# A decoder layer on one core: in the first batch the last four heads' queries come straight from the loaded weights in float32, and GpSimd splits three of the four output weight pieces

## The reference

```python
# 1: attention with 16 query heads, 4 key/value heads, D = 128, window 128
q, k, v = x @ q_kernel, x @ k_kernel, x @ v_kernel      # 256 -> 2048, 512, 512
q, k = apply_rope(q, sin, cos), apply_rope(k, sin, cos)
scores = einsum(q_block, [k_before, k_own]) / sqrt(D), masked
out = einsum(softmax(scores), [v_before, v_own]) @ out_kernel   # 2048 -> 256
x = layernorm(x + out)
# 2: a 256 x 256 attention of the context with itself, applied to x
x = layernorm(x + x_m)
# 3: mixture of experts, 2 shared and 16 routed with the best 4, hidden width 176
x = layernorm(x + moe(x))
```

## Time and profile before

| | us |
|---|---|
| median of 3 runs | 394.87 (394.62 to 395.32) |
| the profiled execution, its own time | 394.55 |
| its span in the profile | 392.8 |
| PE busy | 380.9 (97%) |
| DVE, ACT, POOL busy | 282.9, 264.6, 195.7 |

### The profile page before, as it was taken

One profiled execution on the slowest core, in us unless ns is written; L12 is line 12 of the kernel. 1 busy time (PEld: TensorE's weight loads), 2 busy tenths in 40 slices (PEclk: granted clock), 3 DMA queues, 4 the chain that ended last, 5 costly groups with the idle time before them and its releaser, 6 DMA issues.

```text
span 392.8 us, 8296 instructions
## 1 busy us (share of the span) xinstructions
PE 380.9 (97%) x2520; PEld 342.5 (87%) x2520; DVE 282.9 (72%) x781; ACT 264.6 (67%) x660; POOL 195.7 (50%) x334
## 2 busy tenths in 40 slices
PE   8899899999999999999999999999999999999995
PEld 5767789989999989999998978888889998999995
DVE  4989998778879767978778866765857536645455
ACT  5899887777687777687768785765766644544443
POOL 1598665744777645676546654787856100000000
PEclk9999999999999999999999999999999999999999
DMA  7631500000010000000000494322223222243321
GB/s 262 204 110 48 194 26 4 3 0 3 0 30 0 0 0 0 0 0 0 0 0 1 133 374 163 99 97 81 82 83 94 69 70 78 97 143 99 92 63 53
DMA packets 16709, 28.04 MB, mean 71 GB/s; under 512 B 2198, under 2 KB 7816, under 8 KB 16680
## 3 DMA queue, kind: packets, MB, share of 16 engines
q1 hardware_dynamic: 16248, 27.03, 21.3%
q10 hardware_dynamic: 432, 0.66, 0.5%
HBM read 26.57 MB, written 1.11 MB: 70 GB/s over the span
## 4 chain that ended last, share of the span: by engine, by line
PE 85%; DVE 6%; issue 3%; ACT 2%; POOL 2%; DMA 2%; DVEq 0%; ACTq 0%; POOLq 0%
PE bank L724 22%; PE bank L725 22%; PE bank L726 22%; PE bank L869 6%; PE bank L879 5%; PE bank L868 3%; PE bank L826 2%; PE bank L820 1%; DMA xraw<-in_xt 1%; DVE by_sin L1363 1%; DVE by_cos L1362 1%; POOL nprobs L1600 1%; PE bank L834 1%; DMA raw_q<-in_pieces 1%; POOL nprobs L1599 0%
## 5 line engine op out<-in xcount | busy, mean ns | idle before, releaser
L1030 ACT ACTIVATE hid<-bank,small_sb 128x512 f32<-128x512 f32 x48 | 33.0, 687 | 56.0 <-PE bank L726 47.4
L1250 DVE TENSOR_TENSOR hid<-hid,gate_rows 128x512 f32<-128x512 f32 (+1 forms) x44 | 31.8, 724 | 48.3 <-ACT hid L1030 48.1
L725 PE MATMUL bank<-w_lo,hid_hi 128*128 128x256 f32 (+1 forms) x200 | 56.4, 282 | 0.0
L1591 POOL TENSOR_TENSOR queryT<-by_cos,by_sin 128x512 f32<-128x512 f32 x32 | 41.2, 1287 | 17.1 <-DVE by_sin L1363 16.3
L1599 POOL TENSOR_SCALAR nprobs<-probs,rsums 128x128 f32<-128x128 f32 x64 | 24.5, 383 | 49.6 <-DVE rsums L1379 35.3
L1233 DVE TENSOR_TENSOR hid_lo<-hid,hid_hi 128x512 fp32r<-128x512 f32 x48 | 36.1, 753 | 5.4 <-ACT hid_hi L1051 5.4
L726 PE MATMUL bank<-x2T_hi,w_lo 128*128 128x512 f32 (+1 forms) x100 | 39.5, 395 | 0.0
L725 PEld LDWEIGHTS bank<-w_lo,hid_hi 128*128 128x128 f32 (+1 forms) x200 | 37.7, 188 | 2.0
L869 PE MATMUL bank<-keyT,queryT 128*128 128x256 f32 x128 | 38.2, 381 | 0.0
L724 PE MATMUL bank<-xT_hi,wq_hi 128*128 128x256 f32 x124 | 37.0, 298 | 1.3 <-issue 1.3
L1233 DVE TENSOR_TENSOR pT_lo<-bank,pT_hi 128x384 fp32r<-128x384 f32 x64 | 35.0, 547 | 4.0 <-ACT pT_hi L1126 4.0
(11 more groups left out here) (168 smaller groups left out, 1238.3 us busy)
## 6 DMA issues: line engine op xcount, KB each, us to landing
stage<-in_pieces SPq DMA_DIRECT2D x8, 512.0 KB, 4.3
w_raw<-in_w SPq DMA_DIRECT2D x4, 1024.0 KB, 12.2
gate_rows<-gates_d SPq DMA_DIRECT2D x16, 256.0 KB, 3.1
gate_rows<-gates_d SPq DMA_DIRECT2D x8, 224.0 KB, 3.0
w_raw<-in_w SPq DMA_DIRECT2D x2, 768.0 KB, 7.6
gate_rows<-gates_d SPq DMA_DIRECT2D x8, 192.0 KB, 2.9
gate_rows<-gates_d SPq DMA_DIRECT2D x8, 160.0 KB, 2.4
xraw<-in_xt SPq DMA_DIRECT2D x4, 256.0 KB, 3.1
```

The lines of the kernel that those rows point to most:

```text
L725: nc.tensor.matmul(o, sh, ml, start=False, stop=False, **kw)
L1030: nc.scalar.activation(hid[:, u % 2, :], z_bank[u % 3][:], ACT.Relu, bias=b1_cols[:, i % NC:i % NC + 1]).then_inc(relu_done, 1)
L1250: nc.vector.tensor_tensor(own, own, gate_rows[rows, i % 3, :], ALU.mult).then_inc(gated, 1)
L1591: nc.gpsimd.tensor_tensor(o.rearrange("p a t -> p (a t)"), by_cos[:, r % 2, :], by_sin[:, r % 2, :], ALU.add).then_inc(rope_add, 1)
```

## The change

1. `RAW` gains q6 and q7 (heads 12 to 15). In the first batch each is 4 float32 products of 256 columns of the loaded q3 piece and `xraw`, in place of 12 split products. Other batches still use the split weights.
2. The q3 piece's split moves from between heads 4 and 5 to behind head 8, and its low part goes from POOL to DVE.
3. POOL makes the low parts of o1, o2 and o3, two instructions each; DVE made them before. DVE keeps o0.
4. `load_piece` waits for the raw slots before it loads o3 into q3's buffer, and o3 is loaded after o2. `raw_read` now means q7.
5. The first loads change order (q2 before the second cross transfer), some steps of the first batch change places, and the second warm-up product has 256 columns in place of 384.

```diff
-FIRST_AT = {"act": {"e": 3.719, ..., "piece q3": 4.88, ..., "heads_hi1 0": 9.4995, ...
+FIRST_AT = {"act": {"e": 4.528, ..., "heads_hi1 0": 8.332, ...
-RAW = {"q0": "q0a", "k0": "ka"}
+RAW = {"q0": "q0a", "k0": "ka", "q6": "q3", "q7": "q3"}
-PIECE_AT = {..., "kb": -0.785, ..., "q3": 4.957, "o0": 6.587, "o1": 8.1, "o2": 10.128, "o3": 12.478}
+PIECE_AT = {..., "kb": -0.218, ..., "o0": 6.587, "o1": 7.995, "q3": 8.6, "o2": 8.893, "o3": 12.1}
-LOADS = ["tables", "q0b", "cross 0", "q1", "kb", "cross 1", "q2", "ident", "v", "small", "q3", "o1", "o0", "o3", "o2"]
+LOADS = ["tables", "q0b", "cross 0", "q1", "kb", "q2", "ident", "cross 1", "v", "small", "q3", "o1", "o0", "o2", "o3"]
-LOW_AT = {"v": (2.6, 2.9), "q3": (4.6, 4.8)}
+LOW_AT = {"v": (2.6, 2.9), "o1": (8.6, 9.4), "o2": (10.3, 10.8), "o3": (12.299999999999999, 12.6)}
@@ raw_slot
-            for a in range(2):
+            for a in range(first, first + 2):
                 for k in range(KC):
-                    mm = nc.tensor.matmul(o[:, a * T:(a + 1) * T], w[:, k, a * D:(a + 1) * D], xraw[:, k, :],
+                    mm = nc.tensor.matmul(o[:, (a - first) * T:(a - first + 1) * T], w[:, k, a * D:(a + 1) * D], xraw[:, k, :],
@@ load_piece
+            if n >= 6 and SOURCES[n - 4] in RAW.values():
+                raw_read(sp)
@@ slot on PE
-                    mm = raw_slot(e, o, RAW[s])
+                    mm = raw_slot(e, o, RAW[s], 0 if RAW[s] in HALVES else 2 * (j % 2))
@@
-            keep_busy(512, 384)
+            keep_busy(512, 256)
```

More of the change, by code:

```diff
@@ L114 @@
 }
-FIRST_AT = {"act": {"e": 3.719, "probs_hi 0": 3.077, "q0": -1.712, "v0": 5.9842, "exp 7": 8.009, "exp 8": 8.994, "q3": 0.963, "x": -4.174, "q6": 7.6425, "exp 4": 5.093, "q7": 10.714, "q1": -0.719, "probs_hi 9": 12.249, "q4": 4.991, "v1": 5.765, "k0": -1.004, "probs_hi 7": 10.211, "exp 5": 5.108, "exp 9": 10.073, "probs_hi 4": 6.488, "probs_hi 2": 5.1005, "probs_hi 5": 7.368, "cross 1": 5.9585, "exp 0": 0.87, "piece q3": 4.88, "probs_hi 1": 4.436, "probs_hi 3": 6.212, "piece o1": 8.064, "probs_hi 6": 10.065, "piece o2": 10.371, "exp 1": 1.82, "k1": 1.904, "piece q0b": -1.89, "piece q0a": -2.328, "heads_hi1 0": 9.4995, "piece v": 2.374, "q2": -0.505, "piece ka": -2.22, "exp 6": 7.069, "piece kb": -0.7595}, "dve": {"e": 2.182, "e recip": 2.532, "q0": -1.661, "recip 0": 0.951, "v0": 6.036, "top 0": -0.427, "q3": 1.198, "q6": 8.014, "q4": 4.902, "probs_lo 6": 9.5865, "q7": 10.714, "piece q2": 1.022, "q1": -0.719, "top 4": 2.927, "recip 4": 5.305, "probs_lo 4": 6.596, "top 9": 8.057, "recip 2": 2.516, "probs_lo 9": 12.249, "cross 1": 5.752, "heads_lo1 0": 8.42, "v1": 5.901, "k0": -1.288, "top 6": 5.221, "probs_lo 2": 4.981, "top 2": 1.208, "probs_lo 1": 3.313, "probs_lo 5": 7.706, "top 5": 4.042, "recip 5": 5.306, "top 10": 9.433, "top 1": 0.087, "probs_lo 3": 6.212, "probs_lo 7": 10.025, "recip 1": 1.438, "top 8": 7.617, "recip 8": 8.959, "piece v": 2.059, "heads_lo0 0": 7.37, "k1": 1.847, "probs_lo 0": 2.524, "piece kb": -0.8735, "q2": -0.339, "cross 0": -0.7492, "recip 6": 6.714, "recip 9": 9.5098, "piece o2": 10.09, "top 7": 6.118, "recip 7": 7.833, "piece q0a": -2.857, "recip 3": 3.895}, "pool": {"e copy": -0.151, "normalise 0": 0.494, "q0": -1.555, "k1": 2.094, "q3": 1.95, "normalise 7": 7.651, "q6": 8.0868, "e norm": 4.64, "q7": 10.714, "q1": -0.735, "normalise 9": 9.076, "q4": 5.538, "normalise 4": 4.798, "normalise 3": 2.61, "normalise 1": 1.275, "normalise 8": 9.023, "k0": -1.288, "normalise 2": 2.448, "normalise 5": 5.013, "x": -2.99, "normalise 6": 6.54, "q3 0": 5.4615, "v 1": 2.524, "q2": -0.505, "q5": 7.037}, "pe": {"q0": -1.207, "score 6": 5.0, "v0": 5.866, "q3": 1.371, "q6": 7.899, "e": 3.4688, "score 8": 8.381, "q7": 10.714, "out0 0": 9.857, "q1": -0.719, "v1": 5.807, "turn 9": 12.249, "q4": 4.991, "score 7": 5.01, "values1 0": 9.184, "k0": -1.08, "score 5": 4.312, "score 4": 3.723, "score 2": 2.303, "turn 1": 4.797, "turn 6": 9.096, "score 3": 3.576, "turn 4": 7.014, "turn 2": 5.02, "score 9": 9.122, "turn 5": 7.351, "score 0": 0.11, "score 1": 1.078, "turn 3": 6.212, "cross 1": 2.483, "k1": 1.98, "turn 0": 3.54, "score 10": 9.714, "q2": -0.505, "q5": 7.173, "turn 7": 9.7855}}
@@ new lines @@
+FIRST_AT = {"act": {"e": 4.528, "probs_hi 0": 2.805, "q0": -1.712, "v0": 5.9842, "exp 7": 8.009, "exp 8": 8.994, "q3": 0.963, "x": -4.174, "q6": 7.858, "exp 4": 5.093, "q7": 10.272, "q1": -0.719, "probs_hi 9": 12.249, "q4": 4.991, "v1": 5.765, "k0": -1.004, "probs_hi 7": 10.211, "exp 5": 5.108, "exp 9": 10.073, "probs_hi 4": 6.488, "probs_hi 2": 5.1005, "probs_hi 5": 7.368, "cross 1": 5.9585, "exp 0": 0.87, "probs_hi 1": 4.436, "probs_hi 3": 6.212, "piece o1": 8.064, "probs_hi 6": 10.065, "piece o2": 10.371, "exp 1": 1.82, "k1": 1.961, "piece q0b": -1.89, "piece q0a": -2.328, "heads_hi1 0": 8.332, "piece v": 0.9165, "q2": -0.289, "piece ka": -2.22, "exp 6": 7.069, "piece kb": -0.7595, "q5": 7.413}, "dve": {"e": 2.991, "e recip": 3.341, "q0": -1.661, "recip 0": 0.951, "v0": 6.036, "top 0": -0.427, "q3": 1.198, "q6": 8.229, "q4": 4.902, "probs_lo 6": 9.5865, "q7": 10.272, "piece q2": 1.022, "q1": -0.501, "top 4": 2.927, "recip 4": 5.305, "probs_lo 4": 6.938, "top 9": 8.057, "recip 2": 2.516, "probs_lo 9": 12.249, "cross 1": 5.752, "heads_lo1 0": 8.42, "v1": 5.901, "k0": -1.288, "top 6": 5.221, "probs_lo 2": 4.981, "top 2": 1.208, "probs_lo 1": 3.313, "probs_lo 5": 7.706, "top 5": 4.03, "recip 5": 5.306, "top 10": 9.433, "top 1": 0.087, "probs_lo 3": 6.212, "probs_lo 7": 10.025, "recip 1": 1.438, "top 8": 7.617, "recip 8": 8.959, "piece v": 2.059, "heads_lo0 0": 7.37, "k1": 1.935, "probs_lo 0": 2.252, "piece kb": -0.8735, "q2": -0.123, "cross 0": -0.7492, "recip 6": 6.714, "recip 9": 9.636, "piece o2": 10.09, "top 7": 6.063, "recip 7": 7.833, "piece q0a": -2.487, "recip 3": 3.895}, "pool": {"e copy": 0.658, "normalise 0": 0.494, "q0": -1.667, "k1": 3.228, "q3": 1.95, "normalise 7": 7.859, "q6": 8.302, "e norm": 5.449, "q7": 10.272, "q1": -0.735, "normalise 9": 10.286, "q4": 5.236, "normalise 4": 4.798, "normalise 3": 2.61, "normalise 1": 1.275, "normalise 8": 9.023, "k0": -1.288, "normalise 2": 2.448, "normalise 5": 5.088, "x": -2.99, "normalise 6": 6.54, "q3 0": 5.4615, "v 1": 2.524, "q2": -0.289, "q5": 7.037}, "pe": {"q0": -1.18, "score 6": 5.0, "v0": 5.866, "q3": 1.371, "q6": 8.114, "e": 4.278, "score 8": 9.109, "q7": 10.272, "out0 0": 9.857, "q1": -0.719, "v1": 5.807, "turn 9": 12.249, "q4": 4.991, "score 7": 5.01, "values1 0": 9.122, "k0": -1.08, "score 5": 4.894, "score 4": 3.723, "score 2": 2.303, "turn 1": 4.797, "turn 6": 9.096, "score 3": 3.468, "turn 4": 7.014, "turn 2": 5.005, "score 9": 9.122, "turn 5": 7.351, "score 0": 0.11, "score 1": 0.74, "turn 3": 6.212, "cross 1": 2.483, "k1": 1.98, "turn 0": 3.268, "score 10": 9.714, "q2": -0.289, "q5": 7.223, "turn 7": 10.0645}}
@@ L118 @@
 LATER = {"act": {"y": -0.05, "e": 0.35}, "dve": {"n": -0.5, "m0": -0.75, "m1": -0.25, "y": -0.25}}
 SOURCES = ["q0", "k", "q1", "q2", "v", "q3", "o0", "o1", "o2", "o3"]
-RAW = {"q0": "q0a", "k0": "ka"}
+RAW = {"q0": "q0a", "k0": "ka", "q6": "q3", "q7": "q3"}
 HALVES = {"q0a": ("q0", 0), "q0b": ("q0", 1), "ka": ("k", 0), "kb": ("k", 1)}
-PIECE_AT = {"q0a": -3.638, "ka": -2.057, "q0b": -2.0, "q1": -0.947, "kb": -0.785, "q2": 0.523, "v": 3.345, "q3": 4.957, "o0": 6.587, "o1": 8.1, "o2": 10.128, "o3": 12.478}
+PIECE_AT = {"q0a": -3.863, "ka": -2.057, "q0b": -2.0, "q1": -0.947, "kb": -0.218, "q2": 0.523, "v": 3.345, "o0": 6.587, "o1": 7.995, "q3": 8.6, "o2": 8.893, "o3": 12.1}
@@ L536, in raw_read, with raw_slot @@
             e.wait_ge(projected, max(slot_count(0, s) for s in RAW))
-        def raw_slot(e, o, name):
+        def raw_slot(e, o, name, first):
             e.wait_ge(ld_xt, 16)
```

## The result

The changed kernel took 397.32 us (median of 13 runs, 395.54 to 398.84) against 395.32 us for the kernel before on the same chip (13 runs, 394.62 to 396.06). The ratio is 1.0052, with a 95% interval of 1.0036 to 1.0067: slower by 1.4 to 2.6 us, near +2.05 us. The forecast was +1.4 us. Its 13 runs fall apart: six took 395.54 to 396.48 us, five 398.10 to 398.84, and two lie between, at a mean granted clock of 0.998 to 1.000 in all. The profiled execution, at 397.32 us with a span of 395.5, is one of the two between; before's, at 394.55, was 0.8 us under its median. So the profiles differ by 2.8 us, the medians by 2.0. All ratios here leave out single executions that took far longer (469.84 us of the kernel before beside e9 to e11, 765.06 us of e11).

What follows compares the result with a forecast made beforehand. PE, busy for 97% of the span, was taken as the bound. The shift of the second batch's first product, +1.4 us from two chains that do not add, on 394.87 us gave 396.3 us, range 393.9 to 397.9.

Steps and rivals of the forecast that it cites:

- What bounds: PE bounds; only the first batch can change, and its shift at the second batch's first product (56.89 us) stays to the end.
- Raw slots, +0.54: q6 and q7 on PE as float32 products take 1.72 us each, not 1.45: +0.27 each, +0.54 us.
- The three waits and the new one: PE's waits in heads 3 to 6 shrink, together -2.7 us; a new wait puts values1 at 40.6, leaving 1.2 us lead.
- POOL and DVE: Behind q7, POOL's extra low parts make head 10's transposes 1.4 us late, putting the second batch's first product at 58.3.
- 18.5 us of work for the 16.8 us: Behind q7, POOL gains six low parts, 7.6 us, on top of 10.90 us busy in a 16.80 us stretch.
- The rule of the Trainium skill that was cited: GpSimd shares SBUF interfaces with VectorE and contends with its instructions of two SBUF inputs; instructions reading PSUM are free.
- The next x: Second batch's x queues behind o3 and res, issued at 47.3, landing at 53.9, 7.6 us after the first issue.
- The lower bound: For x's landing: 6.2 us after the first issue, scaled by the bytes queued (1.84 MB against 2.36).
- From x to the first product: After x lands, copy, exponential, hand-over, head 11's normalising and x's low part put the first product at 57.9 to 58.1.
- The two chains don't add: POOL's and x's chains end together at 58.1 to 58.3 against 56.89: +1.2 to +1.4 us, taken once as +1.4.

Runs made afterwards that it cites:

- e9: Changed kernel with the next x issued ahead of o3 and res and the first batch's work reordered on all four engines: 392.50 us, ratio 0.9943.
- e11: Changed kernel with only POOL's rope add for q7 moved back behind head 10's normalising, x still last: 396.24 us, ratio 1.0042.
- e4: Kernel before with only the second warm-up product cut to 256 columns: 395.93 us, ratio 0.9999.
- e6: Kernel before with only q6 and q7 as raw slots, o2 ahead of o3, and the next x ahead of o3 and res: 396.52 us, ratio 1.0011.
- e7: Changed kernel with the next x ahead of o3 and res, and POOL's add for q7 back behind head 10's normalising: 396.25 us, ratio 1.0000.
- e5: Kernel before with only q6 and q7 as raw slots and o2 loaded ahead of o3: 400.49 us, ratio 1.0097.
- e1: Changed kernel with only the second warm-up product back at 384 columns: 397.46 us, ratio 1.0037.
- e2: Changed kernel with only the next x issued ahead of o3 and res: 397.23 us, ratio 1.0033.

## Why the prediction was right in direction and mechanism, and 0.6 us short

- **What bounds.** Right in the main. From the first product of the second batch on, PE's waits are as few as before, but the distance to the end is not unchanged: the shift goes from +2.09 at 58.98 to +2.34 at 68, +2.5 from 164 us and +2.78 at PE's last product. Growth of that size comes up without the change: e4 has a first product only 0.10 us late and is 0.9 late from 157 us on, because three waits for ACT's `xln`, 1.1 us together, came up in it that before's profiled execution lacks.
- **Raw slots, +0.54.** 1.73 us for q7 as worked out; e6 measures 0.4 us (0.0 to 0.8) for both.
- **The three waits and the new one.** values1 of group 0 at 40.6 was forecast and 40.64 measured, the o0 piece 1.31 us (forecast 1.2 to 1.6), q7 44.51 to 46.24 (forecast 44.6 to 46.3).
- **POOL and DVE.** Exponential of head 8 at 43.74, reciprocal at 45.72, head 8 at 47.78, head 9 at 51.77, head 10 at 53.81: each within 0.3 us of the forecast. POOL's rows are the chain that was foretold, without those of the normalisings:

```profile
44.66 2.27 POOL L1655 TENSOR_TENSOR wo_lo<-stage,wo_hi 128x512 fp32r<-128x512 f32 x1
47.69 1.30 POOL L1655 TENSOR_TENSOR wo_lo<-stage,wo_hi 128x512 fp32r<-128x512 f32 x1
49.62 1.29 POOL L1593 TENSOR_TENSOR queryT<-by_cos,by_sin 128x512 f32<-128x512 f32 x1 [0.63 <-DVE by_sin L1365]
```

  The prediction spoke of 18.5 us of work for the 16.8 us of the earlier trace rows. That sum was no cause, since POOL idled for 3.2 us of the same stretch:

```profile
42.40:59.20 16.80, 13.57 (x17) 1.00 0.33 111
```

  0.63 us of that fell between o1's second part and the add for q7, while head 9's normalising stood behind the add. It was order, as e7 shows. The o0 piece (1.31 us for 3.00) and the part of 2.27 us beside DVE's low part of q3 are two more rows of two engines that do not run such instructions together. A third is behind the 0.63 us that POOL idled: the add waited for DVE's second rope product, with both inputs in SBUF, which ran beside o1's second part and took 1.29 us for 0.68, while the first, with one input in PSUM, did not stretch:

```profile
47.64 0.69 DVE L1364 TENSOR_TENSOR by_cos<-bank,tables 128x512 f32<-128x512 f32 x1 [0.24 <-ACT swapped L1105]
48.25 1.29 DVE L1365 TENSOR_TENSOR by_sin<-swapped,tables 128x512 f32<-128x512 f32 x1
```

  The rule of the Trainium skill that was cited (GPSIMD Engine Reference, Key points) agrees with all three. Of the time behind q7 it explains about 1.0 us in the part of 2.27 and 0.6 in the rope product. e7 puts the add's place at 1.44 us (4.59 for 6.03 from head 8 to head 10), the 0.6 included.
- **The next x.** Right in mechanism, and here the size was off. The issues came at 46.43, 46.80 and 47.34 as forecast, but x was split at 54.89 and not at 53.9: it landed 7.5 us after its own issue, near the 8.0 of the earlier trace rows, though there was less ahead of it. SP's queue, for the earlier trace rows:

```profile
46.43 0.33 SPq L568 DMA_DIRECT2D stage<-in_pieces  x1
46.80 0.44 SPq L651 DMA_DIRECT2D res<-in_x  x1
47.34 0.53 SPq L658 DMA_DIRECT2D xraw<-in_xt  x1
```

  The lower bound was also worked out wrongly: the 8.0 us count from x's own issue, but the bytes from the first piece's, at 36.49 in before, from which x took 9.4 us. Scaled from there it is 7.3 us and 53.75. Four profiles have the changed queue (o3, res, x), and x landed 6.4 (e5), 7.5 (changed), 7.9 (e1) and 8.1 us (e11) after its issue; from o3's issue that is 7.4 to 9.0. So the bytes fit e5 and no other. In the changed kernel nearly all of them had moved 2 us before x counted as landed (length, clock, DMA share, GB/s):

```profile
48.00:52.00 4.00, 1.00 1.01 363
53.00:55.00 2.00, 1.00 0.05 14
```

  What holds up the last packets was not found. A spread of 1.7 us at this step is a candidate for that of the 13 runs, but only one of them was profiled, so this is not shown.
- **From x to the first product.** Right. I took the way over x's low part, 4.0 us from x's split; the critical chain above goes that way and takes 4.09. PE's list of waits names another one, since head 11's transposes wait until 58.35 for head 9's low part, which on ACT stands behind x too. It set nothing: in e2, without such a wait, the first product follows those transposes by 0.24 us, here by 0.63, just behind x's low part. The list does not show this rest because the modelled tail of the transposes covers it.
- **The two chains don't add.** Right, as far as e2, e7 and e11 together show: the repaired order alone (e11) wins nothing at the first product of its profile, and with both repairs the loss is gone. They do not end together, though. Without the x chain (e2) the first product comes 1.49 us earlier, of which 0.42 us is an execution that was ahead at q7 already (44.09 against 44.51). So the x chain ended 1.07 us behind POOL's. I had POOL's at 58.3 and x's at 57.9 to 58.1.

So the step that fell short is the term for the landing of x: 53.9 taken, 54.89 measured. The sum went by POOL's chain, 58.3, which ended near 57.9; x's chain set 58.98, 0.7 us more than the forecast. That the runs miss it by nearly the same, +2.05 for +1.4, is in part luck: 0.37 of the 2.09 was there at q2, another 0.7 came up between the first product and the last, and before's profile is 0.8 us under its median.

## What to carry to other kernels

Look at an instruction's place in a busy engine's list before its number: here, with the same six parts on GpSimd and x in time (e2 and e7), the kernel lost 1.3 us more or less by the place of one add, before or behind the normalising that PE needs next. Before a buffer is held longer, look at what is queued behind the load that will reuse it: in e5 the raw slots cost 0.4 us themselves and 3.4 us through an x load queued behind the one that waits for them. And where a change mixes new parts with a new order, try the order on the old parts: here it was worth 2 us without them.

## What the hardware showed beyond that

**A pause of PE costs more than its length.** In e11 PE idled for 2.56 us before head 11 and then ran below full pace. The columns are length, PE busy, granted clock, DMA share and GB/s:

```profile
58.30:59.40 1.10, 0.96 (x6) 1.00 0.00 0
59.40:60.40 1.00, 1.00 (x8) 0.67 0.41 61
60.40:61.40 1.00, 1.00 (x7) 0.50 0.57 201
61.40:62.40 1.00, 1.00 (x5) 0.50 0.00 0
62.40:63.40 1.00, 1.00 (x7) 0.63 0.06 16
```

A granted clock of 0.50 is the lower level, 1.2 GHz. The products resumed at 58.36 at 1.00, and the fall came about 1.4 us later, while PE was busy throughout (0.67 in the second row is 0.66 us at the lower level). It cost 1.6 us: the changed kernel, with its first product at the same 58.98, makes head 12's transposes at 62.59, e11 at 64.17; 1.2 us of that are left at the end (last products at 391.08 and 392.30). Waits of 0.52 us in the changed kernel, of 1.29 and 0.61 us in e5, and of 2.17 us before q2 in e7 had no such sequel. So the profiled execution of e11 ends later than the changed kernel's, while the medians, in ratios, do not differ. Of the other runs of e11 only the mean clock is known; by it two more probably had the fall (397.55 and 398.80 us, at 0.994 and 0.996), but their stretches were not profiled.

**The first raw slot** took 1.81 to 3.23 us in the thirteen profiles, whose kernels all issue the same products there, with a granted clock of 1.00. What makes it longer was not found; it did not follow the length of the warm-up. With the landing of x it is why one profiled span tells little of a change of 1 us here.
